# Order of VectorE's softmax halves in an attention and FFN kernel

## The chip, the cores and the metric

The kernel runs on one core of a Trainium2 chip. The metric is the device time of one execution in microseconds (us); the median of the runs counts.

## The reference, cut to what matters

Sixteen sequences of 100 tokens (1,600 tokens, width 512) pass through a cross-attention layer and a gated FFN, each with a layer norm in front and a residual around it. In the attention each of 16 heads looks at nine neighbouring keys alone, those from `seg_id - 8` to `seg_id`:

```python
scores = (jnp.einsum('bhqd,bkhd->bhqk', q_nope, k_nope) + jnp.einsum('bhqr,bkr->bhqk', q_rope, k_rope)) * scale
k_ids = jnp.arange(lk)[None, None, :]
qs = seg_id[:, :, None]
good = (k_ids <= qs) & (k_ids >= qs - LOOKBACK)
scores = jnp.where(good[:, None, :, :], scores, NEG)
attn = jax.nn.softmax(scores, axis=-1)
out = jnp.einsum('bhqk,bkhd->bqhd', attn, v).reshape(b, lq, H * HD)
return out @ W_o
```

## The kernel before, in words

After a setup, which builds a table of compressed keys and folds the weights of the heads, the 1,600 tokens go through attention in five blocks of 320 tokens (`BLOCKS`), and then through the FFN in four blocks of 400. The loops over blocks of the attention are written out (`unrolled`). The order of work on each engine is written by hand, and the engines meet only through semaphores: `x.wait_ge(sem, n)` holds an engine, and everything behind it on that engine, until the semaphore has reached n.

A block of the attention has three stages. First TensorE makes the queries (`query`, L1079), which VectorE and ScalarE copy out of PSUM. Then comes the softmax stage, which this document is about: eight steps (`STEPS`) of 40 tokens. Last, TensorE multiplies the attended rows by the output weights (`L1227`, `L1232`), 16 heads long.

In a step s of the softmax stage:

- GpSimd multiplies the gathered keys by cosines and sines: `rot_c` (L1005), `rot_s` in two instructions (L1010) and their sum `rot` (L1014). It may run two steps ahead of TensorE's transposes (`tr_mm`).
- TensorE turns the keys (`turn_keys`, L1090 and L1094), puts the mask and the rope part of the scores into PSUM banks 0 and 1 (`mask_and_rope`, L1114 and L1119) and adds the latent part (`latent`, L1128). There is one pair of score banks, so `mask_and_rope` of a step waits on `s_red` until VectorE has reduced the scores of the step before.
- VectorE's `window(b, s)` reads the scores from PSUM: two maxima over the seven places of a row (L1334), the maximum of nine keys (L1338), the subtraction (L1340).
- ScalarE's `exps` takes the exponential (L1252).
- VectorE's `probs(b, s)` sums (L1347), inverts (L1349), multiplies (L1351) and spreads the result over 378 columns with a mask (L1357, `prob_wide`), which raises `pf_ok`. Each of the small results goes to the next instruction through a semaphore of its own.
- TensorE transposes `prob_wide` (`turn_probs`, L1144; it waits on `pf_ok`), ScalarE copies the result (`take_probs`, L1257), TensorE multiplies it by the values (`values`, L1155), and ScalarE copies these back over the queries (`take_values`, L1265).

TensorE runs the scores three steps ahead of the values (`AHEAD = 3`). Its order in its loop over s is: `values(s)`, `mask_and_rope(s + 3)`, `turn_probs(s + 1)`, `latent(s + 3)`, `turn_keys(s + 4)`. In front of the loop stand the scores of steps 0 to 2 and `turn_probs(0)`. VectorE puts `window` and `probs` of one step directly behind each other: 0 and 1 in front of its loop, step s + 2 in turn s.

The layer norm of the next tokens is mixed in. VectorE's `next_norm` makes the variance in turn 3 (L667 to L669) and normalises two tiles in turn 4 and two in turn 5 (L679). TensorE turns tiles 0 and 1 in turn 5 and tiles 2 and 3 in turn 6, behind the other work of these turns (L687), and ScalarE copies them (L696). In the last block they belong to the FFN, whose low parts VectorE takes in the same turns 5 and 6 (`ln_f.low`, L701), waiting for ScalarE's copies.

Of the kernel before, what the change touches and what calls it, by code (L numbers as in the profile page):

```python
# [51 lines left out]
STEPS = 8  # L52
# [33 lines left out]
AHEAD = 3  # L86
# [690 lines left out]
def build_attention(nc, block, ctx, a, w, ffn, ps, ident, table, x1, rows, rowsT, four, low_mass, low_any, ln, ln_f,  # L777
# [10 lines left out]
    def sem(name):  # L788
        return ctx.enter_context(nc.semaphore(name))
# [26 lines left out]
    with ExitStack() as s2:  # L816
# [25 lines left out]
    t_mm, t_ev, s_mm, s_red, mask_ok, s_max, s_sub, s_exp, s_sum, s_inv, s_pn, pf_ok = (  # L842
        sem(s) for s in ("t_mm", "t_ev", "s_mm", "s_red", "mask_ok", "s_max", "s_sub", "s_exp",
                         "s_sum", "s_inv", "s_pn", "pf_ok"))
# [4 lines left out]
    c1, c2, c4, c8, c16, c12, c24 = (Count(n) for n in (1, 2, NLT, STEPS, 16, 12, 24))  # L849
# [17 lines left out]
    def q_bank(o):  # L867
        return o % 4 if o < 20 else o - 16

    def q_dst(o):  # L870
        kind, h = q_out[o]
        return q_lat[:, h % 2, :, h // 2] if kind == "lat" else q_rope[:, :, h]
# [456 lines left out]
    def _(dve):  # L1329
        def window(b, s):  # L1330

            for e in range(2):
                dve.wait_ge(s_mm, c16(b, 2 * s + e + 1))
                dve.tensor_reduce(sc[:, e * GROUPS:(e + 1) * GROUPS, :],  # L1334
                                  ps[:, e, 0:GROUPS * GK].rearrange("p (g q j) -> p g j q", g=GROUPS, q=GQ),
                                  AX.X, ALU.max).then_inc(s_red, 1)
            dve.wait_ge(s_red, c16(b, 2 * s + 2))
            dve.tensor_reduce(mx[:, :], sc[:, :, :], AX.X, ALU.max).then_inc(s_max, 1)  # L1338
            dve.wait_ge(s_max, c8(b, s + 1))
            dve.tensor_tensor(sd[s % 2][:, :, :], sc[:, :, :],  # L1340
                              mx[:, :].unsqueeze(2).to_broadcast([P, E, WIN]),
                              ALU.subtract).then_inc(s_sub, 1)

        def probs(b, s):

            dve.wait_ge(s_exp, c8(b, s + 1))
            dve.tensor_reduce(tot[:, :], ex[s % 2][:, :, :], AX.X, ALU.add).then_inc(s_sum, 1)  # L1347
            dve.wait_ge(s_sum, c8(b, s + 1))
            dve.reciprocal(inv[:, :], tot[:, :]).then_inc(s_inv, 1)  # L1349
            dve.wait_ge(s_inv, c8(b, s + 1))  # L1350
            dve.tensor_tensor(pn[:, :, :], ex[s % 2][:, :, :],  # L1351
                              inv[:, :].unsqueeze(2).to_broadcast([P, E, WIN]),
                              ALU.mult).then_inc(s_pn, 1)
            dve.wait_ge(s_pn, c8(b, s + 1))
            if s >= 2:
                dve.wait_ge(p_mm, c8(b, s - 1))
            dve.tensor_tensor(  # L1357
                pf[s % 2][:, :, :].rearrange("p x (q j) -> p x q j", q=GQ),
                pn[:, :, :].unsqueeze(2).to_broadcast([P, E, GQ, WIN]),
                w["mask"][:, :].rearrange("p (q j) -> p q j", q=GQ).unsqueeze(1)  # L1360
                .to_broadcast([P, E, GQ, WIN]), ALU.mult).then_inc(pf_ok, 1)
# [29 lines left out]
        def body(b, first, last):  # L1391
            if first:
                dve.wait_ge(setup.const_in, 80)
                dve.wait_ge(setup.tab_done, NB)
                dve.wait_ge(setup.front_in, 16)
            for o in range(1, len(q_out), 2):
                dve.wait_ge(q_mm, c24(b, o + 1))
                dve.tensor_copy(q_dst(o), ps[:, q_bank(o), 0:TB]).then_inc(q_dve, 1)
                if o in adds and not first:
                    add_back(dve, b - 1, adds.index(o))  # L1400
                if o in stats(first):
                    next_norm(b, last, stats(first).index(o))
            for s in range(AHEAD - 1):
                window(b, s)
                probs(b, s)
            for s in range(STEPS):
                if s + AHEAD - 1 < STEPS:
                    window(b, s + AHEAD - 1)
                    probs(b, s + AHEAD - 1)
                if NLT <= s + 1 < NLT + 3:  # L1410
                    next_norm(b, last, s + 1)
                if last:
                    for t in tiles_at(s):
                        ln_f.low(dve, 0, t, (2, 3))
            for h in range(RING):
                low_latent(b, h)
            if not last:
                qc.low(dve, b + 1)
            for h in range(RING, H):
                low_latent(b, h)  # L1420
                if last and h % 2 == 1 and (h - RING) // 2 < len(DVE_PARTS):
                    join_bits(dve, DVE_PARTS[(h - RING) // 2], bits_dve)
            if last:
                low_parts()
            dve.wait_ge(o_mm, c16(b, H))
            for m in (1, 3):
                dve.tensor_copy(oT[:, m, :], ps[:, 4 + m, 0:TB]).then_inc(oT_dve, 1)
# [353 lines left out]
```

## Time and profile before

| | |
|---|---|
| median of 3 runs | 741.63 us (740.82 to 750.5) |
| the profiled execution | 743.44 us, of which the span is 741.6 us |
| granted clock of TensorE, mean | 0.996 |
| TensorE matmul busy | 704.4 us (95%) |
| TensorE weight loads busy | 656.4 us (89%) |
| VectorE busy | 431.9 us (58%) |
| ScalarE busy | 380.4 us (51%) |
| GpSimd busy | 207.3 us (28%) |

The span is the time from the first to the last instruction that the profile records; the execution's own time lies 1.8 us above it. In rows of the trace PE is TensorE, PEld its weight loads, DVE VectorE, ACT ScalarE, POOL GpSimd. A row of the timeline merges neighbouring instructions of one line: "x2" and one duration mean two instructions from the first's start to the second's end.

### The profile page before, as it was taken

Reading aid. Unit: us, or ns where it says so; the run is one execution under the profiler, and the core shown is the slowest. Engines: PE = TensorE matmul, PEld = TensorE weight load, DVE = VectorE, ACT = ScalarE, POOL = GpSimd, SP = SyncE. Lnnn points to the kernel's source line nnn. Section 1 sums busy time; section 2 is a strip of 40 time slices with the busy share of each in tenths; the row PEclk is TensorE's granted clock in tenths of the full one; section 3 lists DMA queues with packets and bytes.
Section 4 is the critical chain, followed back from the end, with each engine's and each line's share of the span. In section 5 each row is a group of like instructions: output and inputs, shape, how many; then the busy total and the mean of one; then the engine's idle time right before and its main releaser. Section 6 shows DMA issues by size and latency. Waiting matters only on the chain.

```text
span 741.6 us, 16770 instructions
## 1 busy us (share of the span) xinstructions
PE 704.4 (95%) x6674; PEld 656.4 (89%) x6674; DVE 431.9 (58%) x896; ACT 380.4 (51%) x851; POOL 207.3 (28%) x340
## 2 busy tenths in 40 slices
PE   5899999999999999999999999989999999999996
PEld 5778779879987999779987899779999999999996
DVE  3999946845666547755477446778355253462432
ACT  6778745773458535674357635689232232231230
POOL 1655857504063312605054220640200000000000
PEclk9999999999999999999999999999999999999999
DMA  8999855344304442054313433078471211200301
GB/s 283 342 375 302 276 150 138 86 87 91 97 28 112 91 79 82 15 129 90 90 43 107 86 69 111 3 270 329 180 245 54 72 46 46 66 22 0 103 10 45
DMA packets 47603, 89.93 MB, mean 121 GB/s; under 512 B 5314, under 2 KB 29938, under 8 KB 47522
## 3 DMA queue, kind: packets, MB, share of 16 engines
q1 hardware_dynamic: 40452, 53.67, 26.8%
q0 software_dynamic: 7072, 35.15, 13.9%
q8 instruction: 57, 0.93, 0.5%
q14 instruction: 22, 0.18, 0.1%
HBM read 65.91 MB, written 11.28 MB: 104 GB/s over the span
## 4 chain that ended last, share of the span: by engine, by line
PE 70%; DVE 9%; DMA 6%; SPq 5%; ACT 5%; issue 3%; POOL 2%; DVEq 0%; POOLq 0%
PE ps L1529 17%; PE ps L1079 11%; PE ps L1227 10%; PE ps L1566 8%; PE ps L1232 5%; SPq L961 4%; DMA kv_table<-tab 4%; PE ps L1155 4%; PE ps L1128 3%; PE ps L208 2%; ACT q_lat L1265 2%; PE ps L1090 2%; PE ps L1119 2%; PE ps L1144 1%; DVE prob_wide L1357 1%
## 5 line engine op out<-in xcount | busy, mean ns | idle before, releaser
L1367 DVE TENSOR_TENSOR o_parts<-q_lat,o_parts 128x320 fp32r<-128x320 f32 x80 | 71.7, 912 | 62.4 <-ACT o_parts L1273 62.4
L1227 PE MATMUL ps<-o_parts,wvo_hi 128*128 128x320 f32 x320 | 96.9, 314 | 1.8 <-ACT o_parts L1273 1.8
L1227 PE MATMUL ps<-o_parts,wvo_lo 128*128 128x320 f32 x320 | 95.8, 311 | 0.0
L1273 ACT ACTIVATE o_parts<-q_lat 128x320 fp32r<-128x320 f32 x80 | 65.0, 832 | 44.9 <-PE ps L1227 44.7
L1613 ACT ACTIVATE silu<-ps,ffn_scale 128x400 f32<-128x400 f32 x44 | 26.2, 596 | 105.1 <-PE ps L1529 105.1
L1529 PE MATMUL ps<-ffn_x_lo,ffn_short 128*128 128x400 f32 x352 | 73.8, 346 | 0.0
L1529 PE MATMUL ps<-ffn_x_hi,ffn_short 128*128 128x400 f32 x352 | 71.1, 344 | 0.0
L1651 DVE SCALAR_TENSOR_TENSOR hidden<-ps,ffn_scale,silu 128x400 f32<-128x400 f32 x44 | 27.9, 634 | 70.9 <-ACT silu L1613 63.2
L1005 POOL TENSOR_TENSOR rot_c<-gathered,cosq 128x192 f32<-128x192 f32 x40 | 24.7, 618 | 152.9 <-PE ps L1090 144.0
L1529 PEld LDWEIGHTS ps<-ffn_x_lo,ffn_short 128*128 128x128 f32 x352 | 64.4, 188 | 0.0
L1529 PEld LDWEIGHTS ps<-ffn_x_hi,ffn_short 128*128 128x128 f32 x352 | 64.0, 188 | 0.0
L1227 PEld LDWEIGHTS ps<-o_parts,wvo_hi 128*128 128x128 f32 x320 | 60.8, 190 | 2.3 <-ACT o_parts L1273 2.0
L1227 PEld LDWEIGHTS ps<-o_parts,wvo_lo 128*128 128x128 f32 x320 | 60.4, 189 | 0.3
L1232 PE MATMUL ps<-o_parts,wvo_hi 128*128 128x320 f32 x320 | 60.2, 310 | 0.0
L570 PE MATMUL ps<-wkv,ctx_hi 128*128 128x384 f32 x192 | 52.5, 383 | 2.3 <-DVE wkv L498 2.3
L1232 PEld LDWEIGHTS ps<-o_parts,wvo_hi 128*128 128x128 f32 x320 | 50.7, 189 | 0.0
L1285 ACT ACTIVATE q_lat<-ps 128x320 f32<-128x320 f32 x40 | 32.7, 817 | 29.4 <-PE ps L1079 29.1
L1155 PE MATMUL ps<-probT,gathered 63*128 63x112 f32 x480 | 37.0, 286 | 10.0 <-ACT probT L1257 8.4
L570 PEld LDWEIGHTS ps<-wkv,ctx_hi 128*128 128x128 f32 x192 | 36.0, 196 | 9.7 <-issue 6.7
L1155 PEld LDWEIGHTS ps<-probT,gathered 63*128 63x128 f32 x480 | 30.0, 187 | 16.3 <-ACT probT L1257 10.8
L1014 POOL TENSOR_TENSOR rot<-rot_c,rot_s 128x384 f32<-128x384 f32 x40 | 42.0, 1049 | 3.1
L1265 ACT ACTIVATE q_lat<-ps 128x336 f32<-128x336 f32 x80 | 36.1, 451 | 8.9 <-PE ps L1155 7.5
(161 smaller groups left out, 1566.3 us busy)
## 6 DMA issues: line engine op xcount, KB each, us to landing
gathered<-key_rows SPq DMA_DIRECT2D x240, 47.2 KB
ctx_raw<-ctxT_dram SPq DMA_DIRECT2D x15, 722.0 KB, 9.5
head_w<-head_w_dram SPq DMA_DIRECT2D x16, 576.0 KB, 6.9
ffn_raw<-ffn_w_dram POOLq DMA_DIRECT2D x11, 768.0 KB, 9.7
ffn_short<-ffn_w_dram POOLq DMA_DIRECT2D x11, 768.0 KB, 11.0
kv_table<-tab POOLq DMA_DIRECT2D x16, 288.0 KB, 6.7
rows<-x_dram SPq DMA_DIRECT2D x5, 640.0 KB, 5.1
residual<-x_dram SPq DMA_DIRECT2D x20, 160.0 KB, 2.4
```

What stands on the lines that cost most here:

```text
L570: return pe.matmul(ps[:, 3 * (n % 2) + t, 0:2 * ROW], hi[n % 2][:, c, t * P:(t + 1) * P], wkv[:, c, :], start=(c == 0), stop=(c == KC - 1) ...
L1014: pool.tensor_tensor(rot[s % 2][:, :, :, :], rc[:, :, :].unsqueeze(2).to_broadcast([GR, GROUPS, 2, R]), rs[:, :, :].unsqueeze(2).to_broadc ...
L1079: last = pe.matmul(ps[:, q_bank(o), 0:TB], w[wt][:, hs, :].rearrange("p h c -> p (h c)"), xs[:, :], start=(n == 0), stop=(n == 4))
L1155: last = pe.matmul(ps[:, 6 + side, g * SK:(g + 1) * SK], kvg[keys, s, g, 0:KVC], pt[s % 2][keys, g * SK:(g + 1) * SK], start=True, stop=True)
L1227: last = pe.matmul(ps[:, 4 + m, 0:TB], w[wt][:, h, cols], o_hi[h % RING], start=(h == 0 and n == 0), stop=False, skip_group_check=True)
L1232: last = pe.matmul(ps[:, 4 + m, 0:TB], w["wvo_hi"][:, h, m * P:(m + 1) * P], o_lo[h % RING], start=False, stop=(h == H - 1), skip_group_ch ...
L1265: act.activation(side_tokens(s, side), ps[:, 6 + side, 0:GROUPS * SK].rearrange("p (g e r) -> p g e r", g=GROUPS, e=2), ACT.Copy).then_inc ...
L1273: act.activation(o_hi[h % RING], q_lat[:, h % 2, :, h // 2], ACT.Copy).then_inc(oh_ok, 1)
L1285: act.activation(q_dst(o), ps[:, q_bank(o), 0:TB], ACT.Copy).then_inc(q_act, 1)
L1367: dve.tensor_tensor(o_lo[h % RING], q_lat[:, h % 2, :, h // 2], o_hi[h % RING].bitcast(F32), ALU.subtract).then_inc(ol_ok, 1)
L1529: return pe.matmul(ps[:, 2 * which + c % 2, 0:FT], wt(part, c, which, k), xs, skip_group_check=True, **flags)
L1566: return pe.matmul(ps[:, 4 + m % 2, 0:FT], wt(part, c, 2, m), xs, skip_group_check=True, **flags)
```

## The change

VectorE's order in the softmax stage: `window(b, s + 2)` now stands in front of `probs(b, s + 1)`, instead of `window(b, s + 2)`, `probs(b, s + 2)`. In front of the loop the order becomes window 0, window 1, probs 0, and in the loop window 2, probs 1, window 3, probs 2, and so on; `probs(b, 7)` comes in turn 6, behind `next_norm` of turn 5 and, in the last block, behind `ln_f.low` of tiles 0 and 1. `window` also waits until the subtraction of the window before has been done, since `score` is a single buffer. Number, shape and operands of all instructions stay.

```diff
@@ -1329,6 +1329,8 @@
     def _(dve):
         def window(b, s):
 
+            if b or s:
+                dve.wait_ge(s_sub, c8(b, s))
             for e in range(2):
                 dve.wait_ge(s_mm, c16(b, 2 * s + e + 1))
                 dve.tensor_reduce(sc[:, e * GROUPS:(e + 1) * GROUPS, :],
@@ -1402,11 +1404,13 @@
                     next_norm(b, last, stats(first).index(o))
             for s in range(AHEAD - 1):
                 window(b, s)
-                probs(b, s)
+                if s:
+                    probs(b, s - 1)
             for s in range(STEPS):
                 if s + AHEAD - 1 < STEPS:
                     window(b, s + AHEAD - 1)
-                    probs(b, s + AHEAD - 1)
+                if s + AHEAD - 2 < STEPS:
+                    probs(b, s + AHEAD - 2)
                 if NLT <= s + 1 < NLT + 3:
                     next_norm(b, last, s + 1)
                 if last:
```

## Rows read from the trace of the kernel before

**Rows 1.** Stages by window, block 1: softmax stage, then the stretch to the next.

```profile
core 0: us, PE busy (x) PEld busy (x) DVE busy (x) ACT busy (x) POOL busy (x), PEclk, DMA share, GB/s
...
209.50:240.30 30.80, 28.19 (x625) 23.74 (x619) 22.01 (x74) 21.32 (x54) 15.04 (x25) 1.00 0.25 67
240.30:294.90 54.60, 54.32 (x386) 52.38 (x385) 30.06 (x40) 27.04 (x38) 12.51 (x17) 1.00 0.39 86
```

**Rows 2.** Timeline of VectorE, block 1, step 6: start, duration, instruction, idle before.

```profile
229.88 0.69 DVE L1334 TENSOR_REDUCE score<-ps 128x27 f32<-128x189 f32 x2
...
230.85 0.21 DVE L1340 TENSOR_TENSOR score_shift<-score,score_max 128x54 f32<-128x54 f32 x1
231.38 0.21 DVE L1347 TENSOR_REDUCE exp_sum<-score_exp 128x6 f32<-128x54 f32 x1 [0.31 <-ACT score_exp L1252]
...
231.85 0.21 DVE L1351 TENSOR_TENSOR prob<-score_exp,exp_inv 128x54 f32<-128x54 f32 x1
232.10 0.55 DVE L1357 TENSOR_TENSOR prob_wide<-prob,mask 128x378 f32<-128x378 f32 x1
232.57 0.99 DVE L679 TENSOR_SCALAR rows<-rows,lnq_mv,lnq_rstd 80x512 f32<-80x512 f32 x2
```

**Rows 3.** Timeline of TensorE, block 1, steps of the softmax stage.

```profile
211.78 0.88 PE L1128 MATMUL ps<-key_latT,q_lat 128*56 128x63 f32 x24
...
216.19 0.42 PE L1114 MATMUL ps<-blocks,masks 64*128 64x189 bf16 x2 [0.52 <-DVE score L1334]
...
217.03 0.55 PE L1144 MATMUL ps<-ident,prob_wide 56*63 56x56 f32 x12
...
222.27 0.87 PE L1128 MATMUL ps<-key_latT,q_lat 128*56 128x63 f32 x24
...
225.30 0.55 PE L1144 MATMUL ps<-ident,prob_wide 56*63 56x56 f32 x12
...
229.29 0.88 PE L1128 MATMUL ps<-key_latT,q_lat 128*56 128x63 f32 x24
...
232.81 0.88 PE L1128 MATMUL ps<-key_latT,q_lat 128*56 128x63 f32 x24
...
234.64 0.51 PE L1144 MATMUL ps<-ident,prob_wide 56*63 56x56 f32 x12
...
236.63 0.93 PE L1155 MATMUL ps<-probT,gathered 63*128 63x112 f32 x12 [0.79 <-ACT probT L1257]
```

**Rows 4.** Timeline of GpSimd, block 1, the rotation of keys.

```profile
212.73 1.18 POOL L1014 TENSOR_TENSOR rot<-rot_c,rot_s 128x384 f32<-128x384 f32 x1
...
221.22 1.00 POOL L1014 TENSOR_TENSOR rot<-rot_c,rot_s 128x384 f32<-128x384 f32 x1
223.76 0.59 POOL L1005 TENSOR_TENSOR rot_c<-gathered,cosq 128x192 f32<-128x192 f32 x1 [1.54 <-PE ps L1090]
224.31 0.73 POOL L1010 TENSOR_TENSOR rot_s<-gathered,sinq 128x96 f32<-128x96 f32 x2
225.12 1.00 POOL L1014 TENSOR_TENSOR rot<-rot_c,rot_s 128x384 f32<-128x384 f32 x1
```

**Rows 5.** Timeline of VectorE beside these instructions of GpSimd.

```profile
212.41 0.65 DVE L1357 TENSOR_TENSOR prob_wide<-prob,mask 128x378 f32<-128x378 f32 x1
...
221.24 1.05 DVE L1351 TENSOR_TENSOR prob<-score_exp,exp_inv 128x54 f32<-128x54 f32 x1
...
223.82 0.60 DVE L1340 TENSOR_TENSOR score_shift<-score,score_max 128x54 f32<-128x54 f32 x1
```

**Rows 6.** Timeline of ScalarE, block 1, turn 5.

```profile
235.68 0.90 ACT L1257 ACTIVATE probT<-ps 63x336 f32<-63x336 f32 x2
```

**Rows 7.** Timeline of the last block's end, all engines, rows picked.

```profile
488.26 0.88 PE L1128 MATMUL ps<-key_latT,q_lat 128*56 128x63 f32 x24
...
492.06 0.90 ACT L696 ACTIVATE ffn_x_hi<-ps 128x400 fp32r<-128x400 f32 x2
...
492.60 1.06 DVE L701 TENSOR_TENSOR ffn_x_lo<-ps,ffn_x_hi 128x400 fp32r<-128x400 f32 x2
...
494.84 0.93 PE L1155 MATMUL ps<-probT,gathered 63*128 63x112 f32 x12 [0.51 <-ACT probT L1257]
```

## The prediction

> **What bounds the kernel now.** I read the stages by window first. Outside the softmax stages TensorE never stops (54.32 of 54.60 us busy), inside it is busy for 28.19 of 30.80 us [rows 1]. So whatever moves the end of a softmax stage moves the end of the kernel by the same amount, and the stage has at most 2.6 us per block to give. The timelines of the five blocks agree within some hundredths, so I work out block 1 and count it five times, with a correction for the last.
>
> Next the timelines of TensorE and VectorE in the stage. In the middle TensorE works without a gap, one step in 3.52 us (229.29 to 232.81), and VectorE waits for it. At the opening VectorE's chain is late: the mask product of step 3 starts at 216.19 behind the reduction of step 2. At the end ScalarE's `probT` is late (the values of step 6 at 236.63) [rows 3]. So the reordering can gain at the opening alone; elsewhere the question is whether `probs` now comes too late for TensorE.
>
> **VectorE's step, laid out.** I measure from L, the start of a step's latent scores (L1128), in step 6 L = 229.29 [rows 3]. The two reductions end at 229.88 + 0.69, L + 1.28; this is set by the scores' own end. The subtraction is at 230.85 to 231.06, L + 1.56 to 1.77. Today the sum follows at 231.38, after 0.31 us of waiting for the exponential; `prob` 0.47 behind the sum's start, `prob_wide` 0.25 behind that, 0.55 long [rows 2]. New order: the exponential of the step before is long there, the sum starts about 0.03 behind the subtraction, L + 1.80, and `prob_wide` **of the step before** is ready at L + 1.80 + 0.47 + 0.25 + 0.55 = L + 3.07; TensorE reacts about 0.05 later (`probT` ends at 236.58, the product starts at 236.63 [rows 3, 6]): L + 3.12. So 0.31 us of waiting goes (8 x 0.31 = 2.5 us per block, none of it in front of TensorE in the middle of the stage), but `prob_wide` of step s + 1 moves from in front of `window(s + 2)` to behind it. Nothing is added to VectorE's busy time; the new wait on `s_sub` is for an instruction of its own that ended before, except for window 1 behind window 0, where I put it at 0.03 us, hidden by the wait for scores.
>
> **When TensorE wants it.** `turn_probs(3)` starts at 225.30, L4 + 3.03 with L4 = 222.27 [rows 3]. The new L + 3.12 is 0.09 late. `turn_probs(2)` has slack, since the opening's waits stretch that step. For `turn_probs(4)` and `(5)` this costs 2 x 0.09 = **0.2 us** a block (bounds 0 to 0.3).
>
> **Collisions with GpSimd.** A vector instruction with two SBUF inputs that starts while a GpSimd multiplication or addition runs ends only behind it: subtraction 223.82, 0.60 long instead of 0.21, beside `rot_c` 223.76 to 224.35; `prob` 221.24, 1.05 long, though `rot` had started only 0.02 before it [rows 4, 5]. Reversed, `rot` at 212.73 took 1.18 instead of 1.00 behind `prob_wide` at 212.41. GpSimd's start hangs on TensorE's transposes, so its distance from L4 stays: `rot_c` L4 + 1.49, `rot_s` L4 + 2.04 to 2.77, `rot` L4 + 2.85 to 3.85 [rows 4]. Put VectorE's new chain on it: subtraction held until L4 + 2.15; sum 2.18; `prob` at 2.65, held by `rot_s`, done 2.84; `prob_wide` ready at 2.87, 0.02 behind `rot`. By the pair with 0.02 us GpSimd wins, and `prob_wide` runs its last 0.4 to 0.55 us behind 3.85: done at 4.3, TensorE at L4 + 4.33 instead of 3.03: **+1.3 us**. If `prob_wide` is first it ends at 3.42 and costs 0.45; these are the bounds.
>
> The Trainium skill ("SBUF — State Buffer", "SBUF: two separate sides") says that the pair of ports goes to whichever starts first for its whole instruction; by it the term is 1.3 or 0.45 and nothing between, and the row with 0.02 us agrees with the first.
>
> **The opening.** Scores of step 1 start at 211.78 [rows 3]; subtraction 213.34. `rot`, no longer held by `prob_wide`, runs 212.73 to 213.73 [rows 4], so the subtraction ends at 213.80. Then probs 0: sum 213.83, `prob` 214.30, inside the next `rot_c` (213.90 to 214.50, by the distances of rows 4), done 214.57; `prob_wide` waits for the first `rot_s` (to 214.84) and ends about 215.25. Window 2 starts there instead of at about 215.70, so the mask product of step 3 may start near 215.9 instead of 216.19: the gain. But its subtraction is due at 216.06, inside the next `rot` (about 215.5 to 216.5), ends 216.6; probs 1 needs 0.03 + 1.27: 217.9. `turn_probs(1)` starts at 217.95 and not at 217.03 [rows 3], and the scores of step 3 stand behind it: **+0.9 us** (bounds +0.15 without any collision, for then window 2 starts with its scores and probs 1 ends at 217.13, and 1.2).
>
> **The end of a block.** Last scores L7 = 232.81. `turn_probs(6)` is wanted at 234.64 (L7 + 1.83), for no mask product and scores stand in front of it now, but `probs(6)` comes behind `window(7)`: L7 + 3.12. Part was slack: ScalarE takes `probT` only at 235.68, L7 + 2.87 [rows 3, 6]. New: 3.12 + 0.56 for the transposes = 3.68. The values of step 6 are **0.8 us** later (0.65 to 0.9). `probs(7)` comes behind 0.99 us of normalisation [rows 2]: 3.07 + 0.95 + 1.3 = L7 + 5.3, wanted at about 4.6 + 0.8 = 5.4: hidden, with 0.1 to spare. Layer norm, ScalarE's copies and the tiles' transposes issue as before, in the shadow of these; no DMA is moved on any queue, and SyncE's spreads for the next block follow `av_mm`, that is, TensorE's own shift.
>
> **Last block.** `ln_f.low` of tiles 0 and 1 now stands in front of `probs(7)` and waits for ScalarE, which takes the tiles behind `probT` of step 6. That ends at L7 + 3.68 + 0.90 = 4.58; the low parts start 0.54 behind ScalarE's start and take 1.06 [rows 7]: done at 6.20. `probs(7)` is then ready at 7.50, `turn_probs(7)` at 7.55, `probT` 8.10 to 9.00, the last values at 9.05 instead of 494.84 - 488.26 = 6.58 [rows 7]: **+2.5 us** in the place of 0.8 (bounds 2.0 to 2.9).
>
> **Sum.** An ordinary block: 0.9 + 1.3 + 0.2 + 0.8 = 3.2 us; the last 0.9 + 1.3 + 0.2 + 2.5 = 4.9. Together 4 x 3.2 + 4.9 = 17.7 us. On the profiled execution (743.44 us; 741.6 of it span) that makes 761.1; the median of the runs is 741.63, so 759.3 us. Low ends together: 4 x (0.15 + 0.45 + 0 + 0.65) + 2.6 = 7.6, 749. High ends: 4 x (1.2 + 1.4 + 0.3 + 0.9) + 5.8 = 21, 763. One more collision with a 1.00 us `rot` per block would add up to 5: 768.
>
> **The rivals.**
> - *The collisions fall the other way.* `prob_wide` gets in front of `rot` and the opening's pairs miss each other: 4 x (0.3 + 0.45 + 0.2 + 0.8) + 3.45 = 10.5, 752 us. For it: my distance in step 4 is 0.02 us, and every start hangs on sums of rounded rows. Against it: all five blocks repeat their collisions today.
> - *All is hidden, no change.* If TensorE reaches `turn_probs` later than I lay out, nothing changes but waiting on VectorE: 742 us. Against it: 0.09 us short in every step, and 1.29 short at the end. In the Trainium skill ("Perfetto Trace Analysis", "Identifying the Most-Contended Engine") the engine with the highest occupancy is the one to improve; TensorE's 92% in the stage against VectorE's 71% [rows 1] would by that rule make VectorE's order worth nothing. The rows speak against it, because an order decides by when a result comes.
> - *Faster: the opening decides.* If `probs(1)` ends by 217.0 after all (the price of its delay behind window 2 then nothing), the 0.3 us that the mask product of step 3 gains pass on, and the 0.5 us by which window 2 starts earlier at most: 5 x (0.3 to 0.5) less, 739 us. It decides from the point that `turn_probs(3)` and `(6)` do not wait either; the latter waits 1.29 us by plain program order. Faster by 2% (15 us) asks for more than the 2.6 us x 5 = 13 us that TensorE idles.
> - *Worse.* A further collision per block, or stalls that lower TensorE's granted clock, which is 1.00 in both stretches today [rows 1]: 766 and above.
>
> **How the numbers follow.** Forecast as laid out, 755 to 763: 0.55. Other way, 748 to 755: 0.24. Hidden: 0.07. Faster than before: 0.05. Worse: 0.09. The likeliest gives 759.3 us. The range 750 to 766 leaves out the hidden and the faster case, the fringe of the milder and most of the worse. A 2% difference, about what a measurement of this kernel can tell from no change, lies at 756.5 us: slower by over 2%: 0.55 x 0.93 + 0.09 and little of the milder, 0.63; faster by over 2%: 0.01; the rest, 0.36, within.
>
> **What the profile after would show.** In each block: waiting of L1347 for ScalarE gone; `turn_probs(1)`, L1144, 0.9 us later from the stage's start and its idle time put down to `prob_wide`; `turn_probs(3)` at L4 + 4.3 with a `prob_wide` of 1.4 us beside `rot`; `turn_probs(4)` and `(5)` waiting under 0.2; `turn_probs(6)` waiting 1.3; in the last block `turn_probs(7)` waiting over 2 behind `ffn_x_lo`. The stretch between the stages stays at its length. Wrong would be the forecast if `prob_wide` in step 4 shows 0.55, if `mask_and_rope` waits on reductions in the middle, or if the 30.8 us of the stage stay.

## The result and the profile after

The change makes the kernel slower: 778.91 us (777.89 to 782.12, 4 runs) against 741.75 us (740.82 to 750.5, 4 runs) of the kernel before on the same chip, a ratio of 1.0457 [1.0414, 1.05]. I had forecast 759.3 us and a range of 750 to 766, so the measured time lies outside. The direction was right, but the loss, 37 us, is twice what I had worked out (17.7 us). The profiled execution took 777.89 us; its span is 776.1 us, with a mean granted clock of 0.975 (before: 0.996).

Two lines of the page of the changed kernel, the chain of work that ended last, by engine, and the granted clock in 40 slices:

```profile
PE 77%; DVE 8%; DMA 5%; issue 4%; ACT 3%; POOL 3%; SPq 0%; DVEq 0%; POOLq 0%
...
PEclk9999999979999999999999799997999999999999
```

The second line is the one that I had not reckoned with: in the page of before it is nines throughout. Next the stages by window, of the changed kernel: the softmax stages of blocks 1 and 2, and the stretch behind that of block 2. They answer to [rows 1].

```profile
core 0: us, PE busy (x) PEld busy (x) DVE busy (x) ACT busy (x) POOL busy (x), PEclk, DMA share, GB/s
216.99:254.66 37.67, 30.44 (x613) 25.53 (x607) 21.63 (x74) 20.79 (x53) 15.02 (x25) 0.91 0.25 64
309.81:343.86 34.05, 27.77 (x612) 23.19 (x606) 21.84 (x74) 20.59 (x53) 15.31 (x25) 1.00 0.26 67
343.86:399.00 55.14, 54.91 (x394) 53.14 (x394) 28.86 (x40) 27.25 (x40) 12.28 (x17) 1.00 0.35 81
```

The stage of block 2 in the kernel before:

```profile
294.85:324.74 29.89, 27.27 (x613) 22.93 (x607) 22.00 (x74) 20.58 (x53) 15.05 (x25) 1.00 0.25 71
```

From here on I measure a stage from the start of its first latent scores (L1128) to the start of its last product with the values (L1155); the 30.80 us of [rows 1] also hold that product. The stage is 29.89 to 29.91 us in each of the five blocks before. After, it is 37.03, 37.67, 34.05, 35.45 and 35.29 us. In block 2 all engines are busy for as long as before, within 0.5 us, so the 4.16 us there are waiting. In the other blocks work at the lower clock comes on top: TensorE's busy time in the stage of block 1 is 30.44 us. Block 2, the shortest, has a granted clock of 1.00 throughout; its order can be read without that disturbance. TensorE in block 2 (the latent scores of step 4, not shown, start at 323.48):

```profile
318.24 0.55 PE L1144 MATMUL ps<-ident,prob_wide 56*63 56x56 f32 x12 [1.36 <-DVE prob_wide L1359]
...
327.84 0.55 PE L1144 MATMUL ps<-ident,prob_wide 56*63 56x56 f32 x12 [1.26 <-POOL idx L983]
328.32 0.87 PE L1128 MATMUL ps<-key_latT,q_lat 128*56 128x63 f32 x24
...
331.64 0.26 PE L1114 MATMUL ps<-blocks,masks 64*128 64x189 bf16 x2 [0.79 <-ACT key_ropeT L1244]
...
332.49 0.55 PE L1144 MATMUL ps<-ident,prob_wide 56*63 56x56 f32 x12
...
336.02 0.55 PE L1144 MATMUL ps<-ident,prob_wide 56*63 56x56 f32 x12
...
339.56 0.55 PE L1144 MATMUL ps<-ident,prob_wide 56*63 56x56 f32 x12 [0.51 <-issue]
...
341.11 0.93 PE L1155 MATMUL ps<-probT,gathered 63*128 63x112 f32 x12 [0.30 <-ACT probT L1257]
...
343.86 0.93 PE L1155 MATMUL ps<-probT,gathered 63*128 63x112 f32 x12 [0.79 <-ACT probT L1257]
```

The L1144 rows are `turn_probs(1)`, `(3)`, `(4)`, `(5)` and `(6)`. Measured from the stage's start at 309.81 they stand at 8.43, 18.03, 22.68, 26.21 and 29.75; before they stood at 7.53, 15.80, 19.31, 22.83 and 25.14. The first waits for `prob_wide`, and so does the second. (The row names GpSimd's copy of an index for block 3, but `turn_probs` asks only for the first index of the kernel, and in block 4, where nothing is copied, the same wait of 1.26 us stands.) It starts 4.36 us behind the scores of step 4, where I had worked out 4.33. VectorE and GpSimd in the same block show why:

```profile
325.03 0.60 DVE L1342 TENSOR_TENSOR score_shift<-score,score_max 128x54 f32<-128x54 f32 x1
...
326.36 1.38 DVE L1359 TENSOR_TENSOR prob_wide<-prob,mask 128x378 f32<-128x378 f32 x1
...
329.61 0.35 DVE L1336 TENSOR_REDUCE score<-ps 128x27 f32<-128x189 f32 x1 [1.87 <-PE ps L1128]
330.36 0.35 DVE L1336 TENSOR_REDUCE score<-ps 128x27 f32<-128x189 f32 x1 [0.40 <-PE ps L1128]
```

```profile
326.34 0.99 POOL L1014 TENSOR_TENSOR rot<-rot_c,rot_s 128x384 f32<-128x384 f32 x1
...
328.23 1.05 POOL L191 DMA_INDIRECT key_rows<-kv_table,idx  x1 [0.17 <-issue]
```

`prob_wide` at 326.36 starts 0.02 us behind `rot` at 326.34 and is 1.38 us long, where it was 0.55 alone [rows 2]. That is the collision as forecast. What follows was not forecast: the scores of step 5 start at 328.32, and VectorE's reductions come at 329.61 and 330.36, 1.29 and 2.04 us later. I call such a delay of TensorE's results a lag. In block 4, which has no later block to gather for, the same two reductions start 0.66 us behind the scores, without a gap between them:

```profile
511.17 0.88 PE L1128 MATMUL ps<-key_latT,q_lat 128*56 128x63 f32 x24
```

```profile
511.83 0.61 DVE L1336 TENSOR_REDUCE score<-ps 128x27 f32<-128x189 f32 x2 [1.24 <-PE ps L1128]
```

In block 2 a gather of GpSimd for block 3 starts at 328.23, just ahead. The lag is not the same in every block. In block 0 TensorE also stops in the middle of the scores of step 7 and again in front of `turn_probs(6)`, and the trace shows nothing that it waited for:

```profile
151.55 0.32 PE L1128 MATMUL ps<-key_latT,q_lat 128*56 128x63 f32 x4 [1.54 <-issue]
...
154.06 0.89 PE L1144 MATMUL ps<-ident,prob_wide 56*63 56x56 f32 x12 [1.32 <-issue]
```

And in block 1 there is the clock. Windows there: 241 to 242, before it falls, and those behind it:

```profile
241.00:242.00 1.00, 0.25 (x9) 0.28 (x10) 0.93 (x8) 0.93 (x3) 0.00 (x0) 1.00 1.04 297
242.00:243.00 1.00, 1.00 (x35) 0.94 (x30) 0.25 (x2) 0.63 (x2) 0.70 (x1) 0.90 0.76 235
243.00:245.00 2.00, 2.00 (x14) 1.54 (x12) 1.76 (x8) 1.10 (x4) 0.35 (x1) 0.50 0.89 239
245.00:246.00 1.00, 1.00 (x12) 1.00 (x12) 1.00 (x3) 0.28 (x1) 0.00 (x0) 0.50 0.67 170
246.00:247.00 1.00, 1.00 (x36) 0.66 (x36) 0.25 (x1) 0.62 (x2) 0.00 (x0) 0.89 0.36 70
```

TensorE, which waited in the first of these, has the granted clock 0.50 (1.2 of 2.4 GHz) from 242.8 for 3.4 us. I call this a low stretch. The turning of the keys (L1090) takes 0.90 us in it instead of 0.55, the product with the values (L1155) 1.63 instead of 0.93. Within attention I count such stretches in block 0 (10.2 us, from 31.5 us into the stage), block 1 (3.4 from 8.8, and 3.4 from 25.8), block 3 (10.2 from 31.5) and block 4 (10.2 from 33.5), 37.5 us together; before, one of 3.4 us. Each begins behind one of TensorE's waits: at `turn_probs(1)`, at `(4)`, or at `(6)` and `(7)` at the end of the stage. Those of 10.2 us reach into the next stretch, which is 2.24 us longer behind block 0, 3.04 behind block 3 and 1.54 behind block 4; behind block 2 it has its old length.

### The profile page after: what moved, and what is told of

It reads as the page before. It is cut to its first block, busy times and chain, and to the rows that moved or that the text cites. A ratio compares the mean times of both kernels' runs of the same rounds, so it can differ in the third digit from the quotient of the medians.

```text
span 776.1 us, 16809 instructions
## 1 busy us (share of the span) xinstructions
PE 720.6 (93%) x6674; PEld 669.6 (86%) x6674; DVE 427.5 (55%) x896; ACT 380.3 (49%) x851; POOL 206.9 (27%) x340
## 3 DMA queue, kind: packets, MB, share of 16 engines
q1 hardware_dynamic: 40452, 53.67, 25.8%
## 4 chain that ended last, share of the span: by engine, by line
PE 77%; DVE 8%; DMA 5%; issue 4%; ACT 3%; POOL 3%; SPq 0%; DVEq 0%; POOLq 0%
PE ps L1533 17%; PE ps L1227 12%; PE ps L1079 11%; PE ps L1570 8%; PE ps L1232 6%; PE ps L1155 4%; DMA kv_table<-tab 4%; PE ps L208 3%; PE ps L1128 3%; PE ps L1090 2%; PE ps L1144 2%; PE ps L1119 2%; PE ps L687 1%; PE ps L888 1%; ACT probT L1257 1%
## 5 line engine op out<-in xcount | busy, mean ns | idle before, releaser
L1369 DVE TENSOR_TENSOR o_parts<-q_lat,o_parts 128x320 fp32r<-128x320 f32 x80 | 67.7, 863 | 71.5 <-ACT o_parts L1273 71.5
L1336 DVE TENSOR_REDUCE score<-ps 128x27 f32<-128x189 f32 x80 | 25.3, 349 | 51.4 <-PE ps L1128 49.2
L1257 ACT ACTIVATE probT<-ps 63x336 f32<-63x336 f32 x80 | 35.5, 443 | 29.4 <-PE ps L1144 26.8
L1155 PE MATMUL ps<-probT,gathered 63*128 63x112 f32 x480 | 42.3, 313 | 5.1 <-ACT probT L1257 3.4
L1144 PE MATMUL ps<-ident,prob_wide 56*63 56x56 f32 x480 | 23.2, 230 | 24.2 <-issue 9.8
## 6 DMA issues: line engine op xcount, KB each, us to landing
ffn_short<-ffn_w_dram POOLq DMA_DIRECT2D x11, 768.0 KB, 11.8
```

The lines of the kernel that those rows point to most:

```text
L1144: last = pe.transpose(ps[0:GK, 4 + side, at:at + SR], pf[s % 2][lo:lo + SR, e * GROUPS + g, :], ident[lo:lo + SR, lo:lo + SR])
L1155: last = pe.matmul(ps[:, 6 + side, g * SK:(g + 1) * SK], kvg[keys, s, g, 0:KVC], pt[s % 2][keys, g * SK:(g + 1) * SK], start=True, stop=True)
L1257: act.activation(pt[s % 2][side * HALF:side * HALF + GK, :], ps[0:GK, 4 + side, 0:GROUPS * SK], ACT.Copy).then_inc(p_ev, 1)
L1369: dve.tensor_tensor(o_lo[h % RING], q_lat[:, h % 2, :, h // 2], o_hi[h % RING].bitcast(F32), ALU.subtract).then_inc(ol_ok, 1)
```

## The experiments

Each time stands beside that of the kernel before on the same chip. "Offset" is the distance from the stage's first latent scores.

**1. The added wait alone.** The old order, with the wait on `s_sub` in `window`.

```diff
+            if b or s:
+                dve.wait_ge(s_sub, c8(b, s))
```

> The order of before with the added wait of window on s_sub alone. Theory W (the time goes where TensorE waits for a late prob_wide, and to the lower granted clock behind these waits): the wait is for an instruction of VectorE's own that ended over 1 us before, so 741 to 743 us. Rival V (the new wait delays every window): 40 windows by 0.03 to 0.1 us, up to 4 us if nothing hides them, 743 to 746.

747.55 against 747.47 us, ratio 1.0008 [0.9968, 1.0047]. No difference can be seen, and the stage of block 4 is 29.89 us as before, so everything else lies in the order.

**2 to 5. The order, some steps at a time.** `LATE` names the steps whose `probs` stands behind the next `window`; the changed kernel has all eight, the kernel before none.

```diff
+        def halves(b, s):
+            window(b, s)
+            if s - 1 in LATE:
+                probs(b, s - 1)
+            if s not in LATE:
+                probs(b, s)
```

Steps 2, 4 and 5, those that no forecast collision and no end of a stage touches:

> Window in front of probs for steps 2, 4 and 5 alone; all other steps in the order of before. Theory W: prob_wide of these steps is due within 0.1 us of when TensorE wants it, so 741 to 744 us, and the granted clock stays as before. Rival P (every step whose probs stands behind the next window costs the same share of the 34 us, 1 us each): 15 of 40 steps, 755 us or so.

Steps 0 and 1, the opening:

> Window in front of probs for steps 0 and 1 alone. Theory W: turn_probs(1) waits 1.36 us and stands 0.9 us later per block, 5 x 0.9 = 4.5, so 746 us if the granted clock stays at its higher level, and up to 5 us more in each block in which it falls to 1.2 GHz behind this wait (746 to 760). Rival P: 10 of 40 steps, 750 us with no change in the clock.

Steps 6 and 7, the end:

> Window 7 in front of probs 6, and probs 7 behind the normalisation and, in the last block, behind the low parts of the FFN's tiles; steps 0 to 5 in the order of before. Theory W: the end of each block 0.8 us later, the last 2.5: 4 x 0.8 + 2.5 = 5.7, so 747 us, plus up to 5 us per block in which the granted clock falls. Rival P: 10 of 40 steps... as many as steps 0 and 1, 750 us, and the same as that kernel.

Step 3 alone, the collision:

> Window 4 in front of probs 3 alone; all other steps in the order of before. Theory W: prob_wide of step 3 meets GpSimd's rot and takes 1.38 us, turn_probs(3) waits 1.26 us, and the lag of the next scores seen in blocks 0 to 3 of the changed kernel (0.95 us) comes with it: 5 x 1.3 + 4 x 0.95 = 10.3, so 752 us, plus what the granted clock costs. Rival: the lag belongs to an earlier wait (step 1), then 5 x 1.3 = 6.5 and 748 us.

| steps late | us | kernel before | ratio | change in the stage, order alone | clock |
|---|---|---|---|---|---|
| 2, 4, 5 | 758.16 | 747.47 | 1.0147 [1.0075, 1.0219] | +0.68 (last values) | 0.977 |
| 0, 1 | 755.25 | 747.47 | 1.0136 [1.0048, 1.0224] | +0.91 (`turn_probs(1)` 8.44) | 0.988 |
| 6, 7 | 759.77 | 747.47 | 1.0148 [1.0065, 1.023] | +1.22 (`turn_probs(6)`, block 4) | 0.973 |
| 3 | 763.11 | 744.03 | 1.0237 [1.0193, 1.0281] | +1.33 (`turn_probs(3)` 17.13) | 0.978 |

All four are slower, though no interval lies clear of 2%. The offsets are as forecast where I had one. The times are not: 8 to 19 us are lost where the changes in the stages add up to 3.4 to 6.7 us (with steps 6 and 7 four times 0.78, and 3.39 in the last block, part of it the clock's). Two expectations failed: with steps 2, 4 and 5 I had expected 741 to 744 us and an unchanged clock, and with step 3 some 752 us. The rival that every late step costs the same share fits no better: step 3 alone costs 19 us, more than two or three other steps. Each of the four has stretches at 1.2 GHz (34 us in attention with steps 2, 4, 5 and with step 3, 37.5 with 6, 7, and 17 with 0, 1). The clean case is step 3, block 4 (stage from 485.43), which no gather and no low clock inside the stage disturbs:

```profile
502.56 0.55 PE L1144 MATMUL ps<-ident,prob_wide 56*63 56x56 f32 x12 [1.26 <-issue]
...
516.65 0.59 PE L1155 MATMUL ps<-probT,gathered 63*128 63x112 f32 x6 [0.51 <-ACT probT L1257]
```

Its last product is at 31.22, 1.33 us behind 29.89, exactly the collision. Blocks 0 to 3 of the same run have a further 1.0 us at `latent(6)`.

With steps 2, 4 and 5 late no `turn_probs` up to step 6 waits, as I had expected, yet the last values come 0.68 us late. The timeline of that run shows the way: `window(6)`, `probs(5)`, `probs(6)`, and only then the normalisation that used to start earlier, in block 4 at

```profile
502.67 1.00 DVE L679 TENSOR_SCALAR rows<-rows,lnf_mv,lnf_rstd 100x512 f32<-100x512 f32 x2
503.58 0.61 DVE L1336 TENSOR_REDUCE score<-ps 128x27 f32<-128x189 f32 x2
```

which delays `window(7)` (its reductions come 1.43 us behind the scores instead of 0.67), its exponential and, as I read it, ScalarE's `probT`, which `values(6)` awaits for 1.31 us. So it was too little to say that the middle has 0.09 us per step to lose: a `probs` moved out of one turn fills the next.

**6. Without the collision.** GpSimd's `rot_c` of steps 5 and 7 waits for `prob_wide`.

```diff
+            if s in (5, 7):
+                pool.wait_ge(pf_ok, c8(b, 2 if s == 5 else 4))
```

> The changed kernel, with GpSimd's rotation of step 5 also waiting for prob_wide of step 1 and that of step 7 for prob_wide of step 3, so that they no longer run beside VectorE's two-input instructions. Theory C (half of the loss is the shared collisions with GpSimd): turn_probs(3) waits about 0.1 instead of 1.26 us, turn_probs(1) 0.7 less: 5 x (1.2 + 0.7) = 9.5 less, plus the lag of 3.8 if it hangs on this wait, plus most of the clock's 14: 752 to 769 us. Rival O (the order itself, not the collision): no less than 776 us, since GpSimd's rotations are now later.

763.44 against 744.03 us, 1.0261 [1.021, 1.0312], some 15 us of the 37 regained. `turn_probs(1)` stands at 7.79 (0.26 over before instead of 0.90) and `(3)` at 16.08 (0.28 instead of 2.23). So the whole term of step 3 and 0.64 of the 0.90 us at the opening are collisions with GpSimd. What remains is in part low clock (mean 0.977) and, in blocks 0 to 3, this, from TensorE's timeline of block 2:

```profile
322.10 0.43 PE L1130 MATMUL ps<-key_latT,q_lat 128*56 128x63 f32 x8
...
322.88 0.39 PE L1130 MATMUL ps<-key_latT,q_lat 128*56 128x63 f32 x6 [0.35 <-issue]
...
323.61 0.50 PE L1130 MATMUL ps<-key_latT,q_lat 128*56 128x63 f32 x10 [0.34 <-issue]
```

The 24 matmuls of `latent(6)`, 0.88 us in one run in block 4, fall into three pieces, the second and the third behind a pause in which the trace shows nothing that TensorE waited for. Block 4 of this run has no such thing. Of the blocks, 0 to 3 alone gather keys for a next one.

**7. The gathers behind the square roots.** GpSimd's square roots for the layer norm (`ln.root`) first, then the two gathers.

```diff
+                ln.root(pool, b + 1)
                 gather(b + 1, 0)
                 gather(b + 1, 1)
-                ln.root(pool, b + 1)
```

> The changed kernel, with GpSimd's first two indirect gathers of the next block behind its root for the layer norm instead of in front of it, some 4 us later. In blocks 0 to 3 of the changed kernel TensorE's results of step 5 reach the other engines up to 1.4 us late while these gathers start, and in block 4, which has none, they do not. Theory G (the gathers cause that lag): it goes or moves to where it costs less, up to 4 x 0.95 = 3.8 us less, 775 us. Rival: it comes from TensorE itself after the wait of 1.26 us: stays at L + 1.3 and L + 2.0 for the two reductions, 779 us.

775.02 against 744.03 us, 1.0409 [1.0368, 1.045]. The time hardly moves, as expected, but the place does. The two gathers start at 23.5 and 25.2 us into the stages of blocks 2 and 3 instead of 18.4 and 19.9; there `latent(6)` is now at 22.05, as in block 4, and the lag shows up at `values(5)` instead, 27.55 against 26.62 in block 4. The lag follows the gathers.

**8 and 9. The clock, held up by filling.** While TensorE waits, it multiplies constants into columns of a PSUM bank that nobody reads; the result is not used. First in three places, then in all.

```diff
+            for _ in range(times):
+                pe.matmul(ps[:, bank, 384:512], w["other"][:, :], w["blocks"][:, 0:P], start=True, stop=True,
+                          skip_group_check=True)
...
             if s >= 1:
                 pe.wait_ge(p_ev, c16(b, 2 * s))
+            fill(5, TURNS.get((b, s), TURNS.get(s, 0)))
             pe.wait_ge(pf_ok, c8(b, s + 1))
```

> The changed kernel, with 8, 10 and 8 small matmuls on constants into unused columns of PSUM in front of TensorE's wait for prob_wide of steps 1, 3 and 6; their results are read by nobody. Theory K (waiting of TensorE lowers the granted clock, and the clock costs some 14 us): the waits are filled, the clock's stretches at 1.2 GHz go or get fewer and 765 to 772 us come out, though TensorE does more work. Rival: the clock falls for another reason (load of the other engines, temperature, DMA): 779 us or more.

769.65 against 744.03 us, 1.0341 [1.0299, 1.0382], clock 0.989. With 8, 10 and 8 of them before `turn_probs(1)`, `(3)` and `(6)` the low stretches shrink to 3.4, 3.4 and 10.2 us.

> The changed kernel with small matmuls on constants in all of TensorE's longer waits: in front of prob_wide of steps 1 (10), 3 (20), 6 (15) and, in the last block, 7 (32), in front of the values of steps 6 (4) and 7 (12), and 10 larger ones in the gap before the last block's output product. Theory K (the granted clock falls because TensorE waits): no stretch at 1.2 GHz inside the attention, blocks as long as block 2 of the changed kernel, so 742 + 5 x 4.2 + 2 less what the last gap gave away, 761 to 765 us. Rival: the clock's stretches stay, 770 or more.

768.13 against 744.98 us, 1.028 [1.0242, 1.0319]. From the view of cores, and the windows of the stages of blocks 1 and 2:

```profile
core 0: 764.3 us, clock 0.996
```

```profile
214.44:249.22 34.78, 31.26 (x674) 26.34 (x667) 21.86 (x74) 20.69 (x53) 15.34 (x25) 1.00 0.26 67
304.38:338.43 34.05, 31.25 (x674) 26.34 (x668) 21.87 (x74) 20.59 (x53) 15.33 (x25) 1.00 0.23 65
```

One low stretch of 3.4 us is left in attention, in block 0, behind a wait of 0.84 us at `turn_probs(4)` that comes with the lag. TensorE has 62 matmuls more in block 2's stage than in the changed kernel, and the stage is as long, 34.05 us; the kernel as a whole is about 11 us faster than the changed one (11.8 us by the two spans). It is slower than the 761 to 765 us that I had expected. Work that serves nothing shortens the kernel, and the clock is what it chiefly changed (0.975 to 0.996). The stages of blocks 1 and 3 are 34.78 and 34.77 us at full clock, so the lag is larger there than in block 2.

**10. The same filling in the kernel before.** 12 in front of `values(6)` and `(7)`, and 10 in the last gap.

> The kernel before with 12 such matmuls in front of the values of steps 6 and 7, and 10 larger ones in the last gap. Theory K: before has one stretch at 1.2 GHz, 3.4 us behind the 1.8 us gap of the last block, and other runs of it up to 10 us more; filled, 739 to 741 us and a smaller spread. Rival (the fills delay what they wait beside): 743 or more.

742.72 against 744.98 us, 0.9955 [0.9932, 0.9978]: the 3.4 us at 1.2 GHz behind the last block are gone, and the medians lie 2.3 us apart. Compared filled with filled, on one chip, the changed order costs 768.13 - 742.72 = 25 us, and 23.4 us by the two traces. Of these, 17.0 are the order's own waits (worked out below), 4.6 what the lag takes more in the changed order than in the old one, and 1.5 the low stretch that is left.

**11. Only the opening changed, filled.** `LATE = (0, 1)`, `rot_c` of step 5 behind `prob_wide` of step 1, and in turn 0 TensorE does the scores of step 3 and `values(0)` before `turn_probs(1)`; ScalarE's two copies of that turn change places too (not shown). The filling is that of experiment 10.

```diff
+                if s == 0:
+                    latent(b, AHEAD)
+                    values(b, 0)
                 if s + 1 < STEPS:
                     turn_probs(b, s + 1)
-                if s + AHEAD < STEPS:
+                if s and s + AHEAD < STEPS:
                     latent(b, s + AHEAD)
-                if s == 0:
-                    values(b, s)
```

> The filled kernel before, plus a new opening: window in front of probs for steps 0 and 1 alone, TensorE's scores and values of step 3 and 0 in front of turn_probs(1), ScalarE's copies in the same order, GpSimd's rotation of step 5 behind prob_wide of step 1. By the offsets measured, values(1) starts 10.55 us behind the first scores instead of 10.87: 5 x 0.3 = 1.6 us less than the filled kernel before, 737.5 to 739.5. Rival: probs(2) now comes late for turn_probs(2), no gain or a loss of up to 1 us a block.

740.41 us (738.78 to 743.54, 9 runs) against 744.98, 0.9931 [0.9899, 0.9962]. TensorE in block 2, whose stage starts at 295.06:

```profile
301.80 0.88 PE L1130 MATMUL ps<-key_latT,q_lat 128*56 128x63 f32 x24
302.61 0.93 PE L1168 MATMUL ps<-probT,gathered 63*128 63x112 f32 x12
303.37 0.51 PE L1154 MATMUL ps<-ident,prob_wide 56*63 56x56 f32 x12
...
305.36 0.81 PE L1168 MATMUL ps<-probT,gathered 63*128 63x112 f32 x10 [0.68 <-ACT probT L1275]
```

`turn_probs(1)` at 303.37 waits for nothing, since the scores and values that stood behind it are in front. The second product comes at 10.30 instead of 10.87, so the opening gains 0.57 us in four of the blocks and 0.27 in block 3. At the end of the stage this is 29.40 instead of 29.99 us in block 4, against experiment 10; in blocks 0 to 2 it is 0.4 to 0.6, in block 3 nothing. It is faster than the kernel before by 0.7%, a little less than I had expected (737.5 to 739.5 us). The intervals of experiments 10 and 11 overlap: that the reordering helps beyond the filling is read from the offsets, not from the times.

**12. No collision, filled.** Experiments 6 and 9 together, with less filling (4 and 2 matmuls) at `turn_probs(1)` and `(3)`, where the waits are shorter.

> The changed order with GpSimd's rotations of steps 5 and 7 moved off VectorE's chain, and TensorE's waits filled. What is left is the order's own price: 0.25 at the opening, 0.3 at step 3, 0.8 at the end (2.5 in the last block), and the lag beside the gathers of about 1 us in four blocks: 742 + 5 x 0.55 + 4 x 1.8 + 2.5 = 754 us. Rival: 763 us as without the fills, if the clock does not hang on TensorE's waits.

755.82 against 744.98 us, 1.0122 [1.0086, 1.0157], clock 0.997. What is left of the loss, 11 us, is the end of each stage, what the waits of GpSimd cost, and the gathers.

**13. All gathers behind the last product.** Experiment 9, with GpSimd waiting for `av_mm` before it loads the indices.

```diff
+                ln.root(pool, b + 1)
                 pool.wait_ge(tick, Count(WSETS)(b, 1))
+                pool.wait_ge(av_mm, c8(b, 8))
                 load_index(b + 1)
                 gather(b + 1, 0)
                 gather(b + 1, 1)
-                ln.root(pool, b + 1)
```

> The changed order with TensorE's waits filled, and the first two gathers of the next block held until the last values of the stage. Theory G (the gathers' start holds TensorE up): steps 4 to 7 of blocks 0 to 3 run at the offsets of block 4, values(7) of blocks 0 to 3 at 33.1 us behind the first scores instead of 34.0 to 36.2, 761 to 764 us in all unless the later rows hold up the next block's queries. Rival: the lag stays at step 5 (latent of step 6 at 23.2 or more instead of 22.0).

819.25 against 745.54 us, 1.099 [1.0938, 1.1042], far from the 761 to 764 us expected: the next block's rows and keys now come late, which makes each stretch between the stages 15 to 17 us longer. The stages themselves are what the experiment was for. TensorE in block 2, scores of steps 5 and 6 of a stage that starts at 329.21:

```profile
347.63 0.87 PE L1129 MATMUL ps<-key_latT,q_lat 128*56 128x63 f32 x24
...
351.21 0.88 PE L1129 MATMUL ps<-key_latT,q_lat 128*56 128x63 f32 x24
...
362.11 0.93 PE L1167 MATMUL ps<-probT,gathered 63*128 63x112 f32 x12
```

The offsets are 18.42 and 22.00, where the changed kernel had 18.51 and 23.16 in its block 2. Block 4 of this run, and of experiment 9, has 22.00 and 21.97. The last product is at 32.90, 32.88 and 32.90 in blocks 0 to 2; block 3 opens 0.28 us late for another reason and ends at 33.18. So the order alone costs 32.90 - 29.89 = 3.01 us. With the gathers in the stage and at full clock, the stage was 34.05 in block 2 of the changed kernel and 34.78 and 34.77 in blocks 1 and 3 of experiment 9: the lag is 1.15 to 1.9 us a block.

**14 and 16. The last block.** `probs(7)` directly behind `probs(6)`, in front of the normalisation and `ln_f.low`; first with all the filling, then without the 32 matmuls before the last block's `turn_probs(7)`.

```diff
-                if s + AHEAD - 2 < STEPS:
+                if s + AHEAD - 2 < STEPS - 1:
                     probs(b, s + AHEAD - 2)
+                if s + AHEAD - 2 == STEPS - 2:
+                    probs(b, STEPS - 1)
```

> The changed order with TensorE's waits filled, and probs 7 right behind probs 6, in front of the normalisation and the low parts. The prediction's term for the last block: turn_probs(7) no longer waits for ffn_x_lo, so values(7) of block 4 at 33.1 instead of 34.9, 1.7 to 1.8 us less in all; in blocks 0 to 3 the normalisation of tiles 2 and 3 comes 1.3 us later and may hold TensorE's transposes up to 1 us each. 763 to 770 us against 768. Rival: no difference anywhere.

768.34 us, 1.0294 [1.0236, 1.0352], and `turn_probs(7)` of block 4 at 32.89 as in experiment 9 (32.91). Inconclusive, for the 32 matmuls of filling take 1.96 us in front of it and set its start themselves.

> As the run with probs 7 directly behind probs 6, but without the 32 small matmuls in front of turn_probs(7) of the last block. By the prediction's term, turn_probs(7) of block 4 then starts at about 31.0 us behind the first scores instead of 32.9, and values(7) at about 33.1 instead of 34.9: 1.7 us less, 766 to 767 us. Rival: turn_probs(7) is held by something else (the reading of the tiles), 32.9 again.

766.45 against 744.59 us, 1.0269 [1.0196, 1.0342]. TensorE in block 4, stage from 486.66:

```profile
517.55 0.51 PE L1152 MATMUL ps<-ident,prob_wide 56*63 56x56 f32 x12
...
519.64 0.93 PE L1166 MATMUL ps<-probT,gathered 63*128 63x112 f32 x12
```

`turn_probs(7)` is at 30.89, where I had expected 31.0, and the last product at 32.98 instead of 34.90. So what stands in front of `probs(7)` costs 1.9 us there. In blocks 0 to 3, where this is the normalisation alone, `turn_probs(7)` does not move (32.8 in blocks 0 and 3, as in blocks 1 and 3 of experiment 9); the 1.9 us are those of `ln_f.low`. They agree with the changed kernel, where `turn_probs(7)` of block 4 waits for 1.92 us.

**15. The best version without gathers in the stage.** Experiment 11 with the edit of 13.

> The filled kernel before with the new opening, and the first two gathers behind the last values. In its form with the gathers in the stage, blocks 0 to 3 lag 0.5 us beside them. Theory G: 4 x 0.5 = 2 us less, 738 to 740 us. Rival: rows, residuals or gathered keys of the next block come late, since SyncE's queue stands behind the gathers: slower, 745 or more.

798.65 against 745.54 us, 1.0712 [1.0672, 1.0753]. I had expected 738 to 740 us. The stages come out clean and alike, 29.31 to 29.33 us in blocks 0 to 3, but the next block starves as in experiment 13. In this form it is no gain.

## Why the prediction failed, though its terms held

**The terms of the order, which I had worked out, held.** The opening was +0.90 us (forecast 0.9). Step 3 was +1.33 (forecast 1.3), by `prob_wide` held behind `rot`, as the pair with 0.02 us had let me expect. Steps 4 and 5 cost 0.03 to 0.13 (0.2). The end of a block cost 0.75 to 0.78 (0.8). The last block's `probs(7)` cost 1.9 on top of these; I had put 2.5 in place of 0.8, so 1.7. Together, from experiments 13 and 9, 4 x 3.01 + (34.90 - 29.89) = 17.0 us; forecast 17.7. The wait on `s_sub` cost nothing, as I had put it. Of the middle I had overlooked that the moved `probs` fills the next turn (experiment 2); the 3.01 us of the whole change leave no room for such a term.

**The step that failed** is the sum, which took every other time for unchanged, and with it the sentence "the stretch between the stages stays at its length". It put two terms at nothing: the time that TensorE loses at the lower clock, which the runs show as some 11.8 us, and the lag of TensorE's results, some 7.7 us. The trace also has one of the signs of being wrong that I had named, a wait of `mask_and_rope` in the middle: in block 2 the mask product of step 6 waits for 0.79 us behind late results.

*The granted clock.* I had it as a rival with a chance of 0.09 and no price ("stalls that lower TensorE's granted clock"), though the trace of before had a price to offer. Its one low stretch of 3.4 us begins behind the gap at the end of attention:

```profile
497.61 0.64 PE L1227 MATMUL ps<-o_parts,wvo_hi 128*128 128x320 f32 x1 [1.84 <-ACT o_parts L1273]
```

From this product to the twentieth behind it 4.42 us pass, in experiment 10, where the gap is filled, 3.02: 1.4 us lost. After, the five stages are 13.0 us longer than the order alone makes them (32.90 us, 34.90 in the last block). Not all of that is the clock. In blocks 0 and 3 it falls only at 31.5 us into the stage, and by then `turn_probs(6)` is already 2.9 and 1.8 us late against experiment 13. In block 1 the scores of step 6 come 1.8 us late at full clock. With the 1.15 of block 2 these are 7.7 us of lag, which leaves 5.3 for the clock inside the stages. The stretches behind them are 6.5 us longer together. That makes 11.8 us, and filling the waits in experiment 9 gave back 11 to 12. In the Trainium skill ("TensorE: Matmul & The Clock Gate", "The HAM clock gate") idleness is what drops TensorE from 2.4 to 1.2 GHz. The trace agrees that the clock falls behind waits; those in front of the five low stretches of the changed kernel are 0.79 to 1.92 us long.

*The lag.* It is 1.15 us in block 2, 1.8 in blocks 1 and 3 and 2.9 in block 0, and nothing in block 4. With the gathers moved out of the stage it is gone from every block (experiment 13). The old order has it too: in experiment 1 `latent(6)` comes 0.7 us late in blocks 2 and 3, in experiment 10 `latent(7)` 0.4 to 0.5 us late in blocks 0 to 3, never in block 4. The execution that I predicted from showed none of it.

The sum: 17.0 + 7.7 + 11.8 = 36.5 us; the start of the kernel, which varies from run to run, was 1.9 us shorter, and the spans differ by 34.5. The medians lie 37.2 us apart, for the profiled execution of before was 1.7 us slower than its median, and that of after 1.0 us faster.

**The rivals.** The collisions did not fall the other way, nothing was hidden, and the opening did not gain while its collision stood; without it, and with TensorE's own order changed, it gained 0.57 us a block at `values(1)` (experiment 11). "Worse" won, by the second of its two conditions.

**What stays open.** Which block the clock falls in: block 2 was spared, and of the five equal waits at `turn_probs(1)` the clock fell behind that of block 1 in the changed kernel, and behind those of blocks 2 and 4 in experiment 3. How a gather holds up TensorE: in experiment 6 it issues in pieces, in the changed kernel its recorded start is on time and its results are late. I can only show that the lag follows the gathers and is gone without them in the stage; that the pause of 1.54 us in block 0, 8 us behind the last gather's start, belongs to them too is not shown by itself. Busy DMA engines alone are not enough: block 4 has none of the lag, though the weights of the FFN load at the same place in its stage (DMA share 0.76 to 1.04 from 511 us on). Whether TensorE's own instructions arrive late in these pauses was not tested. And the price of the clock is a difference between blocks and between kernels, not a measurement of its own.

## What to carry to other kernels

Moving a step back by one place in an in-order queue costs what the step's result is late by, and that could be worked out here to within 0.2 us a term from one trace, collisions between VectorE and GpSimd included. But where a change adds waits to TensorE, the sum needs a second term: ask of the trace of before whether the granted clock has already fallen behind a gap, and price low stretches as a second case of the forecast (here 1.4 to 1.5 us for each 3.4 us of dense work, 11.8 us on top of 17.0). One trace of before is also not enough to say what is steady: the lag was missing from it and was there in others. The check of the clock afterwards is cheap: fill the waits with matmuls that nobody needs, and see what comes back.

## What the runs showed of the hardware

- TensorE's low stretches (granted clock 0.50, 1.2 GHz) lasted 3.4 to 17.1 us in attention. In the softmax stages they began behind waits of 0.7 to 1.9 us; the kernel with no added wait at `turn_probs` up to step 6, and 0.68 us more per stage (experiment 2), had 34 us of them in attention.
- A `prob_wide` that starts 0.02 us behind a GpSimd addition takes 1.38 us instead of 0.55.
- In stages with gathers of GpSimd (1.05 us each), TensorE's issue or the arrival of its results lagged by 0.4 to 2.9 us, with no wait in the trace that accounts for it.
- Filling matmuls (128 columns, bf16, 0.06 us each) in TensorE's waits took the mean granted clock from 0.975 to 0.996 and the kernel from 779 to 768 us.
- The clock varies from run to run in the unchanged kernel too: on one chip 12 runs of it took 741.89 to 751.69 us, with mean granted clocks from 0.999 to 0.983.
